# A routed feed-forward block on one core: shared blocks ahead of the routed tiles, routed results scattered with addition

## The reference

```
x = x + attn(layernorm(x))           # attn: B x, scan h = a*h + Bu, C h + D*x
n = layernorm(x)
shared = (silu(n Wg') * (n Wu')) Wd'
logits = n gate_w' ;  e = argmax(logits) ;  s = sigmoid(max(logits))
routed = (silu(s n Wg[e]') * (s n Wu[e]')) Wd[e]'
out = x + shared + routed
```

## Time and profile before

| | us |
|---|---|
| median of three runs | 280.43 (279.65 to 280.50) |
| the profiled execution as a run | 279.88 |
| its span in the trace | 277.6 |
| mean granted clock of PE | 0.957 |

### The profile page before, as it was taken

How to read it: one execution, slowest core, us unless ns; L and a number is a source line. 1 busy time by engine, 2 the same in 40 slices (tenths; PEclk the granted TensorE clock), 3 DMA queues, 4 the chain that set the end, 5 groups by cost and what they waited for, 6 DMA issues and landing times. The chain is left out here.

```text
span 277.6 us, 6124 instructions
## 1 busy us (share of the span) xinstructions
PE 233.6 (84%) x1891; PEld 181.1 (65%) x1891; DVE 179.9 (65%) x512; ACT 173.0 (62%) x415; POOL 146.2 (53%) x150
## 2 busy tenths in 40 slices
PE   0584988878779999999997699999999999999900
PEld 0263655565367466676774599999999999765700
DVE  3599998799887986559873156666666666644200
ACT  2753988996997984643342686777767676723400
POOL 1000000017777777778770027777777777775940
PEclk9999597999999999999999799999999999999975
DMA  6999500002323223232853923655465543211991
GB/s 210 396 333 327 218 0 0 2 1 101 116 100 119 100 106 110 100 117 97 284 206 105 297 99 93 167 170 172 132 176 165 143 121 96 72 47 50 107 175 22
DMA packets 24862, 37.83 MB, mean 136 GB/s; under 512 B 3680, under 2 KB 16864, under 8 KB 24272
## 3 DMA queue, kind: packets, MB, share of 16 engines
q1 hardware_dynamic: 15264, 22.03, 26.0%
q0 software_dynamic: 9568, 15.41, 19.9%
HBM read 22.03 MB, written 19.73 MB: 150 GB/s over the span
## 5 line engine op out<-in xcount | busy, mean ns | idle before, releaser
L1045 POOL DMA_INDIRECT table<-rows,place x64 | 65.6, 1024 | 60.2 <-DVE place L808 41.1
L1086 POOL DMA_INDIRECT out<-w_full x51 | 49.5, 970 | 33.5 <-DVE w_full L1022 19.5
L1015 DVE SCALAR_TENSOR_TENSOR hid<-bank,h_scale,n1T 128x512 f32<-128x512 f32 (+1 forms) x39 | 27.4, 703 | 29.8 <-ACT n1T L657 28.4
L440 PE MATMUL bank<-xT_hi,w_split 128*128 128x256 f16 (+1 forms) x156 | 40.9, 264 | 0.8 <-DVE xT_lo L1007 0.5
L442 PE MATMUL bank<-xT_hi,w_split 128*128 128x256 f16 (+1 forms) x156 | 40.9, 264 | 0.0
L441 PE MATMUL bank<-xT_lo,w_split 128*128 128x256 f16 (+1 forms) x156 | 40.7, 263 | 0.0
L452 PE MATMUL bank<-w_full,hid 128*128 x284 | 38.7, 277 | 0.1
L587 ACT ACTIVATE n1T<-bank,g_scale 128x512 f32<-128x512 f32 x32 | 21.8, 687 | 23.3 <-PE bank L394 23.1
L452 PEld LDWEIGHTS bank<-w_full,hid 128*128 128x128 f32 x284 | 34.8, 192 | 1.4 <-issue 0.2
L406 PEld LDWEIGHTS bank<-w_full,hid 128*128 128x128 f32 x256 | 32.4, 200 | 1.8
L406 PE MATMUL bank<-w_full,hid 128*128 128x128 f32 x256 | 32.6, 283 | 0.0
(11 more groups left out here) (142 smaller groups left out, 432.6 us busy)
## 6 DMA issues: line engine op xcount, KB each, us to landing
w_full<-table SPq DMA_DIRECT2D x24, 264.0 KB, 3.0
rows<-in_x SPq DMA_DIRECT2D x8, 512.0 KB, 7.8
w_full<-in_weights SPq DMA_DIRECT2D x3, 1152.0 KB, 12.7
table<-in_pads SPq DMA_DIRECT2D x1, 2112.0 KB, 10.5
table<-in_pads SPq DMA_DIRECT2D x8, 264.0 KB, 4.2
x_ring<-table SPq DMA_DIRECT2D x8, 264.0 KB, 3.3
out<-rows POOLq DMA_DIRECT2D x8, 256.0 KB, 7.8
table<-rows,place POOLq DMA_INDIRECT x64, 2.4
```

The source lines that it names most:

```text
L440: mm(o, w_of(kind, e, 0, c), xT_hi[k][:, 0:w], start=True, stop=False)
L1015: v.scalar_tensor_tensor(out=hid[j % 4][:, 0:w], in0=up_bank[j % 2][:, 0:w], scalar=h_scale[:, 0:1], in1=silu[j % 2][:, 0:w], op0=ALU.mult ...
L1045: g.indirect_dma_start(table[:, :], bass.IndirectOffsetOnAxis(ap=place[:, i:i + 1], axis=0), rows[:, i, :], None).then_inc(done, 16)
L1086: g.indirect_dma_start(out[:, :], bass.IndirectOffsetOnAxis(ap=x_in[k][:, s, 2 * D:2 * D + 1].bitcast(I32), axis=0), x_in[k][:, s, 0:D], N ...
```

## The change

- All 16 shared blocks run ahead of the routed tiles, in the order of their sequences; `base` on DVE adds each to `x1`. `late_base` and `add_late` are gone.
- SP stores each finished block plainly to the output (16 DMAs of 256 KB): blocks 0 to 8 ahead of the pads, 9 to 11 behind them, 12 to 15 between the loads of tiles 3 and 4.
- Rows of the table hold the second norm, the number and the logit alone (`TILE_ROW` = 136 numbers). They are scattered without waiting for any block's `base`. Pads and tile loads have the same narrow rows.
- `routed_result` copies from PSUM instead of adding. `scatter_result` adds to the output (`compute_op=ALU.add`); POOL waits ahead of the first for all 16 stores.
- On ACT, score and scale of tiles 0 and 1 stand in the shared loop, behind the Silus of block 14.

```diff
...
@@ -82,7 +79,7 @@
     def stored(k, j):
         return 16 * sum(halves(i) for i in range(k, j, XRING))
 
-    table = nc.dram_tensor("table", (E * REGION + E * SLOTS, ROW), F32, kind="Internal").ap()
+    table = nc.dram_tensor("table", (E * REGION + E * SLOTS, TILE_ROW), F32, kind="Internal").ap()
 
     with ExitStack() as ctx:
         def sb(name, shape, dtype=F32):
...
@@ -284,19 +276,30 @@
                 row = nc.sync.snap(row_reg[e % 2], min_val=0, max_val=E * REGION - SLOTS)
                 sp.dma_start(table[bass.ds(row, SLOTS), :], pads[e * SLOTS:(e + 1) * SLOTS, :]).then_inc(s_padded, 16)
 
+            def store_block(b):
+                sp.wait_ge(s_base, b + 1)
+                sp.dma_start(out_tiles[:, b * BT:(b + 1) * BT, :], x1[:, b * BT:(b + 1) * BT, :]).then_inc(s_out, 16)
+
+            for b in range(9):
+                store_block(b)
             sp.wait_ge(s_map, 1)
             for e in range(E):
                 store_pads(e)
+            for b in range(9, 12):
+                store_block(b)
             sp.wait_ge(s_wlo, 2 * 2)
             sp.wait_ge(s_map, MAP)
             sp.wait_ge(s_dummy, 16)
             sp.wait_ge(s_padded, 16 * E)
             for k in range(4):
-                sp.wait_ge(s_first_rows[k], 16 * LATE * BT // 4)
-                sp.wait_ge(s_scattered[k], 16 * EARLY * BT // 4)
-            for j in range(TILES):
+                sp.wait_ge(s_scattered[k], 16 * NT // 4)
+            for j in range(4):
                 load_tile(j)
-            sp.wait_ge(s_out, 16 * LATE)
+            for b in range(12, BLOCKS):
+                store_block(b)
+            for j in range(4, TILES):
+                load_tile(j)
+            sp.wait_ge(s_out, 16 * BLOCKS)
 
         @block.tensor
         def _(pe):
...
@@ -444,6 +446,8 @@
 
             def routed_down(j):
                 pe.wait_ge(r_hid, j + 1)
+                if j < 2:
+                    pe.wait_ge(s_base, BLOCKS - 1 + j)
                 after(pe, r_out, j - 1)
                 for s in range(halves(j)):
                     o = down_bank[j % 2][:, P * s:P * (s + 1)]
...
@@ -500,14 +504,12 @@
             pe.wait_ge(s_wlo, 4)
             load_expert(0)
             transpose_tile(0)
-            shared_down(FIRST - 1)
             transpose_tile(1)
-            pe.wait_ge(s_silu, FIRST * FC)
-            pe.wait_ge(s_hid, FIRST * FC)
+            shared_down(BLOCKS - 1)
+            pe.wait_ge(s_silu, BLOCKS * FC)
+            pe.wait_ge(s_hid, BLOCKS * FC)
             for j in range(TILES):
                 routed_gate_up(j)
-                if j == 0:
-                    pe.wait_ge(s_late, MIDDLE)
                 if j >= 1:
                     routed_down(j - 1)
                 if j + 2 < TILES:
...
@@ -515,17 +517,7 @@
                 if j + 1 < TILES:
                     load_expert(j + 1)
 
-            for b in range(FIRST, BLOCKS):
-                if b == FIRST:
-                    pe.wait_ge(r_silu, TILES)
-                    pe.wait_ge(r_hid, TILES)
-                shared_gate_up(b)
-                if b == FIRST:
-                    routed_down(TILES - 1)
-                    pe.wait_ge(r_out, TILES)
-                if b > FIRST:
-                    shared_down(b - 1)
-            shared_down(BLOCKS - 1)
+            routed_down(TILES - 1)
 
         @block.scalar
         def _(act):
...
@@ -666,20 +649,17 @@
                     split_hi(LAST, 1)
                 if b in (4, 5):
                     routed_weights_hi(b - 4)
-                if EARLY < b < FIRST - 1:
-                    late_base(b - 1)
-
-            tile_score(0)
-            tile_scale(0)
-            tile_scale(1)
-            late_base(FIRST - 2)
+                if b == BLOCKS - 2:
+                    tile_score(0)
+                    tile_scale(0)
+                    tile_scale(1)
+
             tile_hi(0)
+            tile_hi(1)
             tile_score(2)
             tile_scale(2)
-            tile_hi(1)
             tile_scale(3)
-            late_base(FIRST - 1)
-            act.wait_ge(s_hid, FIRST * FC)
+            act.wait_ge(s_hid, BLOCKS * FC)
             for j in range(TILES):
                 routed_silu(j)
                 if j % 2 == 0 and j + 4 < TILES:
...
@@ -688,14 +668,6 @@
                     tile_hi(j + 2)
                 if j + 4 < TILES:
                     tile_scale(j + 4)
-
-            act.wait_ge(r_hid, TILES)
-            for b in range(FIRST, BLOCKS + 1):
-                if b < BLOCKS:
-                    shared_silu(b * FC, 0)
-                    shared_silu(b * FC + 1, 1)
-                if b > FIRST:
-                    late_base(b - 1)
 
         @block.vector
         def _(dve):
...
@@ -975,12 +947,10 @@
                 map_ready(v.tensor_scalar(tile_weights[:], tile_expert_f[:], float(F), None, ALU.mult))
                 assert map_steps[0] == MAP
 
-            for b in range(1, FIRST + 1):
-                if b < FIRST:
-                    shared_hidden(b * FC, 0, b)
-                    shared_hidden(b * FC + 1, 1, b)
-                if 1 <= b <= EARLY:
-                    base(b - 1)
+            for b in range(1, BLOCKS):
+                shared_hidden(b * FC, 0, b)
+                shared_hidden(b * FC + 1, 1, b)
+                base(b - 1)
                 if b == 1:
                     places(GROUPS - 2)
                 if b == 3:
...
@@ -1017,14 +987,13 @@
 
             def routed_result(j):
                 n = halves(j)
-                own = x_in[j % XRING][:, 0:n, 0:D]
                 dve.wait_ge(r_o, j + 1)
-                v.tensor_tensor(out=own, in0=down_bank[j % 2][:, 0:P * n].rearrange("p (s d) -> p s d", s=n), in1=own,
-                                op=ALU.add).then_inc(r_out, 1)
-
-            dve.wait_ge(s_o, FIRST)
+                v.tensor_copy(x_in[j % XRING][:, 0:n, 0:D],
+                              down_bank[j % 2][:, 0:P * n].rearrange("p (s d) -> p s d", s=n)).then_inc(r_out, 1)
+
             tile_lo(0)
             tile_lo(1)
+            base(BLOCKS - 1)
             for j in range(TILES):
                 routed_hidden(j)
                 if j >= 1:
...
@@ -1043,7 +1009,7 @@
             def scatter_row(i, done):
                 pool.wait_ge(s_place, i // GT + 1)
                 g.indirect_dma_start(table[:, :], bass.IndirectOffsetOnAxis(ap=place[:, i:i + 1], axis=0),
-                                     rows[:, i, :], None).then_inc(done, 16)
+                                     rows[:, i, D:ROW], None).then_inc(done, 16)
 
             g.memset(ones_f[:], 1.0).then_inc(s_ones, 1)
             g.memset(rows[:, :, 2 * D:ROW], 0.0).then_inc(s_rowset, 1)
...
@@ -1069,37 +1035,26 @@
                 if q < PAIRS and turn == 14:
                     pool.wait_ge(s_bu, min(q + 3, PAIRS))
 
-            for i in range(LATE * BT):
+            for i in range(NT):
                 keep_step(i)
-                scatter_row(i, s_first_rows[i % 4])
-            for b in range(EARLY):
-                pool.wait_ge(s_base, b + 1)
-                for t in range(BT):
-                    if t == 2 and b + 2 < FIRST:
-                        pool.wait_ge(s_u, (b + 3) * FC)
-                    scatter_row(block_of(b) * BT + t, s_scattered[t])
+                b = i // BT - BLOCKS // 2
+                if b >= 0 and i % BT == 2:
+                    pool.wait_ge(s_u, (b + 3) * FC)
+                scatter_row(i, s_scattered[i % 4])
 
             def scatter_result(j):
                 k = j % XRING
                 pool.wait_ge(r_out, j + 1)
                 for s in range(halves(j)):
                     g.indirect_dma_start(out[:, :],
-                                         bass.IndirectOffsetOnAxis(ap=x_in[k][:, s, 2 * D:2 * D + 1].bitcast(I32), axis=0),
-                                         x_in[k][:, s, 0:D], None).then_inc(s_stored[k], 16)
-
-            def add_late(b):
-                n = block_of(b)
-                pool.wait_ge(s_late, b - EARLY + 1)
-                g.dma_start(out_tiles[:, n * BT:(n + 1) * BT, :], x1[:, n * BT:(n + 1) * BT, :],
-                            accum_op=ALU.add).then_inc(s_out, 16)
-
+                                         bass.IndirectOffsetOnAxis(ap=x_in[k][:, s, D:D + 1].bitcast(I32), axis=0),
+                                         x_in[k][:, s, 0:D], None, compute_op=ALU.add).then_inc(s_stored[k], 16)
+
+            pool.wait_ge(s_out, 16 * BLOCKS)
             for j in range(TILES):
                 scatter_result(j)
             for k in range(XRING):
                 pool.wait_ge(s_stored[k], stored(k, TILES))
-            for b in range(EARLY, BLOCKS):
-                add_late(b)
-            pool.wait_ge(s_out, 16 * LATE)
 
 
 def kernel(L0_attn_x, L0_attn_A, L0_attn_B, L0_attn_C, L0_attn_D, L0_ffn_gate_w, L0_ffn_shared_gate,
...
```

More of the change, by code:

```diff
@@ L18 @@
 ROW = 264
+TILE_ROW = 136
 PITCH = 66
@@ L28 @@
 ROUTE = 5
-LATE = 8
-MIDDLE = 5
 GROUP = 2
@@ L172, in block_kernel @@
```

(33 more changed lines are left out.)

5 lines of the change are left out of this document (removed).

## The result

| | before | after |
|---|---|---|
| run, median | 280.47 us (four runs) | 315.76 us (four runs) |
| ratio, 95% interval | | 1.1265 (1.1234 to 1.1295) |
| profiled span | 277.6 | 313.7 |
| first result scatter starts | 164.43 | 175.33 |
| from one result scatter to the next, mean of 70 | 1.274 | 1.858 |

The change makes the kernel 35 us slower; 274.4 was forecast. The three differences in the table sum to the difference of the spans: +10.9 for the later start, +40.9 for the spacing (70 x 0.584), -15.7 at the end, +36.1 in all.

A forecast was written before the change was run, and what follows sets the result against it. POOL's queue was taken to bound the routed stage: first result scatter 174.7, plus 89.2 to the last, 3.1 landing and 5.1 to the end give span 272.1, run 274.4 us; range 270.0 to 288.4.

The forecast's parts named there:

- wait at the tanh of tile 4: Hand-over to routed tiles: ScalarE waits 2 to 3 us for loads 4 and 5, landed at about 171.2.
- landing of an adding scatter: End of the kernel: the last accumulating scatter takes 3.1 us to land, followed by 5.1 us to the end.
- price of the accumulating result scatter on POOL: Routed stage: POOL's extra time per adding scatter, taken as 0, bounded by 0 and +0.41 us each.
- rival A: Routed stage: accumulating scatters cost POOL more; half the upper bound, 0.2 us each, gives 288.4 us; chance 0.38.
- The point at which it turns the sign: Routed stage: extra POOL time per adding scatter at which the gain becomes a loss, put at 0.08 us.
- The rule of the Trainium skill: Adding scatters: two read descriptors per chunk; half of 0.97 us more each would add 34 us, giving 308.
- POOL as the bound: Routed stage: POOL needs 2.55 us a whole tile, other engines 2.41, so POOL's queue decides.
- Blocks into the hole: Between shared and routed stages: three blocks, 13.1 us, delay the first routed matmul only +6.8 us, at full clock.
- the plain stores, the additions of DVE and the later pads: Shared stage: DVE's additions cost 0; first nine stores and delayed pads finish in time, with 2 us to spare.
- the stall's price: Hand-over: loads 4 and 5 behind the last stores delay POOL's first result scatter by 3.5 us, from 171.2 to 174.7.
- The ring of 12 tiles: Routed stage: loading tile j + 12 after tile j's result lands costs 0, with slack over 3 us.
- The copy on DVE: Routed results: a copy from PSUM replaces the addition and leaves POOL's scatter at 0.97 us.

The follow-up runs named there:

- e1: Changed kernel with its result scatters made plain again, nothing else changed: 274.62 us, ratio 0.9834 to the kernel before.
- e3: Separate kernel only issuing DMAs from POOL, plain and adding, indirect and direct: adding costs an indirect scatter 0.59, 0.52, 0.46 us more at 128, 64, 32 rows.
- e6: Changed kernel with plain result scatters and the loads of tiles 4 to 7 ahead of the stores of blocks 12 to 15: 270.54 us, ratio 0.9693.
- e9: Changed kernel, loads of tiles 4 to 7 ahead of the stores of blocks 12 to 15, only 16 of 71 result scatters adding: 280.32 us, ratio 1.0017.
- e4: Changed kernel with the loads of tiles 4 to 7 ahead of the stores of blocks 12 to 15: 311.55 us, ratio 1.116 to the kernel before.
- e5: Kernel before with MIDDLE = 6, so that 14 shared blocks run ahead of the routed tiles: 278.26 us against 279.53, ratio 0.9955.
- e7: Kernel before with MIDDLE = 6 and LATE = 7, so 14 blocks ahead and seven late blocks: 280.15 us, ratio 1.002.

## Why the prediction was wrong, point by point

| step | forecast | measured |
|---|---|---|
| first routed matmul | 166.2 | 165.48 |
| wait at the tanh of tile 4; its start | 2 to 3 us; 171.2 | 4.2 us; 171.31 |
| first result scatter | 174.7 | 175.33 |
| spacing | 1.274 | 1.858 |
| last result scatter | 263.9 | 305.41 |
| landing of an adding scatter | 3.1 | 3.3 |
| last start to the end | 8.2 | 8.3 |
| run | 274.4 | 315.76 |

- **The step that failed** is the price of the accumulating result scatter on POOL. I took 0, with an upper end of +0.41 us; it is +0.58, beyond the end, 40.9 us over 70 spacings. The mechanism was the one named as rival A, with the right sign, but it was sized at +0.2 and given less weight than the forecast, so that 315.76 lies beyond the whole range. The point at which it turns the sign was put at 0.08 us each; e1, with a span 5.1 us under that of the kernel before, gives 0.07.
- **Why the bound was none.** I took the shortest direct adding store, 1.383 us for 512 rows, as the most that an indirect one of 128 rows could take. e3 shows that the two kinds are not on one scale: an indirect scatter of 128 rows costs 0.96 against 0.56 for a direct one, and adding puts 0.59 on it against 0.33. A limit from another form of instruction bounds nothing. I read the row as "little per row, so little in all"; what is dear is the instruction, not the row (e3: 0.42 of 0.59), and that one row, without a plain store beside it, could not show.
- **The rule of the Trainium skill** (Collectives: The Full Stack, two read descriptors where a copy has one), by which I worked out 308 us and which I then set aside, was nearer than my row: half more was too little, 60% more is measured. But its reason does not carry the size here: an extra that follows the number of descriptors would fall with the rows, and at 32 rows, a quarter of them, it is still 0.46 us.
- **POOL as the bound** of the routed stage, which the busy share of 53% hides, was right: e1, e6 and e9, worked out ahead from POOL's queue alone, came out within 0.6, 0.1 and 0.3 us.
- **Blocks into the hole** was right (+6.1 for +6.8), and so was that ScalarE would wait at tile 4, though for longer (4.2 us for 2 to 3). That the plain stores, the additions of DVE and the later pads cost nothing fits the sum (e1 lands at 274.62) but no run took them out one by one. The start of that tanh, 171.31 for 171.2, is in part luck: the load of tile 5 is issued at 168.30 and not 168.9, and takes 2.9 us and not 2.2. e4 and e6 show the stall's price, 4.1 us for the 3.5 forecast, and start POOL at 171.31 and 171.24, where 171.2 was forecast without the stall. The clock did fall in the wait, 0.50 in 172 to 174, which I had taken as 0; from the tanh to POOL's start it is 4.0 us for the 3.5 forecast.
- **The ring of 12 tiles** was counted with a spacing of 1.27. With 1.86 it does starve the engines before POOL, 40.6 us of waits on ScalarE, without a cost, as POOL is later still.
- **The copy on DVE** holds POOL up nowhere: 0.96 for each scatter in e1, which bears out what the two pages of the Trainium skill that the prediction names for it say.

## What to carry to other kernels

Before a plain scatter is turned into an adding one, find out whether the queue that issues it is the bound, by the spacing of its instructions and not by its busy share; if it is, the price is the difference per instruction times their number, whatever is saved elsewhere. An operation that no trace shows has to be measured alone before a change rests on it, and its price must not be bounded by an instruction of another form. A change of several parts is best taken apart: one block moved into the wait, and nothing else, gained half a per cent (e5); all three were moved only together with the new kind of scatter, whose price swallowed the gain. All three ahead, with the plain scatters and the accumulating stores of before, was not run.

## What the runs showed of the hardware

- On POOL an indirect scatter of 128 rows takes 0.96 us and one with addition 1.55; with 0.30 between two that is 1.26 and 1.86. At 32 rows it is 0.86 and 1.32. The size of a row changes neither (plain: 128, 512 and 1056 bytes; adding: 128 and 512).
- A plain scatter is 32 packets on POOL's DMA queue at 128, 64 and 32 rows, an adding one 144, 80 and 48 (e3).
- Direct stores from POOL: 0.56 us plain and 0.88 adding for 128 rows, 0.76 and 1.30 for 512.
- An adding scatter of 64 KB lands 3.3 us after its start, a plain one 2.2 (medians in the changed kernel and in e1).
- TensorE's granted clock fell to its lower level about idle stretches of 4.1 us (before, mean 0.56 in the 3.9 us that follow), 3.3 us (after, 0.50 from 172 to 178) and 2.7 us (e7, 0.73 and then 0.50 in the 4 us that follow).
